# Expert outputs scattered with addition into two sums, and transposes and products sized by an expert's tokens

## What is computed

```python
logits = x @ gate_w.T; scores = softmax(logits)
topk_w, topk_ids = top_k(scores, K);  topk_w /= topk_w.sum(-1)
buf[e, pos] = x[tok]                       # up to CAP = 256 tokens of an expert, the rest is dropped
g, u = split(buf @ w13);  eo = (silu(g) * u) @ w2
routed[tok] += eo[e, pos] * topk_w         # four terms for each of the 1024 tokens
out = residual + routed + (silu(x @ sh_gate) * (x @ sh_up)) @ sh_down
```

## Time and profile before

| | us |
|---|---|
| median of 3 runs | 205.45 (204.16 to 205.67) |
| span of the profiled execution | 228.0 |
| head, to the first product of an expert | 0 to 82.1 |
| expert stage on PE | 82.1 to 197.5 |
| last scatters on POOL and their landing | 197.5 to 203.4 |
| tail: load, sums, stores | 203.4 to 228.0 |

### The profile page before, as it was taken

The page is one execution under the profiler, slowest core; times in us unless marked ns, Lnnn a source line. Parts: engine busy times, 40 slices in busy tenths (PEclk is TensorE's granted clock), DMA queues, the critical chain, the costliest instruction groups (busy, mean ns, idle before and its releaser), DMA issues.

```text
span 228.0 us, 3659 instructions
## 1 busy us (share of the span) xinstructions
PE 139.5 (61%) x819; PEld 119.8 (53%) x819; DVE 120.4 (53%) x385; ACT 84.8 (37%) x254; POOL 115.6 (51%) x140
## 2 busy tenths in 40 slices
PE   1124887787774879969895948858499479200000
PEld 0112765676663559959794837837398377100000
DVE  2878999997433344555253531536237055303990
ACT  3165678566563024434214231335225032002410
POOL 6201156888877500754563736555464646632740
PEclk9999996555555799988999788999979958755555
DMA  5999999998222264775775657465665731129930
GB/s 173 334 340 340 338 339 364 365 373 301 96 99 95 95 198 134 235 204 153 218 198 176 192 161 220 136 189 158 185 172 171 232 115 52 43 69 359 385 122 23
DMA packets 40270, 46.46 MB, mean 204 GB/s; under 512 B 4585, under 2 KB 37045, under 8 KB 40252
## 3 DMA queue, kind: packets, MB, share of 16 engines
q1 hardware_dynamic: 35200, 37.30, 53.2%
q0 software_dynamic: 4608, 8.54, 10.5%
q10 hardware_dynamic: 444, 0.40, 0.5%
HBM read 27.95 MB, written 22.45 MB: 221 GB/s over the span
## 4 chain that ended last, share of the span: by engine, by line
PE 36%; issue 20%; SPq 19%; another core or an unknown queue 7%; DVE 7%; DMA 5%; ACT 2%; POOL 0%; POOLq 0%; ACTq 0%; DVEq 0%
PE bank L882 18%; PE bank L899 11%; SPq L204 10%; PE bank L874 8%; SPq L227 5%; DVE part L769 4%; DMA G<-rows_out 3%; DVE act_t L730 1%; ACT xT L476 1%; DMA xg<-rows_in 1%; ACT sg L481 1%; DVE res L769 1%; SPq L210 1%; DMA rows_out<-yo,pick_idx 1%
## 5 line engine op out<-in xcount | busy, mean ns | idle before, releaser
L333 POOL DMA_INDIRECT rows_out<-yo,pick_idx x64 | 62.6, 978 | 55.7 <-issue 47.8
L882 PE MATMUL bank<-xT,w13b 128*128 128x128 f32 x368 | 51.6, 294 | 8.5 <-issue 5.6
L882 PEld LDWEIGHTS bank<-xT,w13b 128*128 128x128 f32 x368 | 48.1, 208 | 11.0 <-issue 11.0
L476 ACT ACTIVATE xT<-bank,cols 128x256 f32<-128x256 f32 x64 | 26.8, 473 | 43.0 <-PE bank L874 37.0
L899 PE MATMUL bank<-w_all,act_t 128*128 128x256 f32 x92 | 29.7, 434 | 16.0 <-DVE act_t L730 14.9
L730 DVE TENSOR_TENSOR act_t<-sg,bank 128x256 f32<-128x256 f32 x32 | 13.5, 421 | 49.3 <-ACT sg L481 36.5
L318 POOL DMA_INDIRECT rows_in<-n_row,slot_all x32 | 32.5, 1015 | 10.0 <-issue 10.0
L481 ACT ACTIVATE sg<-bank 128x256 f32<-128x256 f32 x32 | 12.3, 386 | 44.6 <-PE bank L882 25.1
L899 PEld LDWEIGHTS bank<-w_all,act_t 128*128 128x128 f32 x92 | 16.5, 209 | 18.8 <-issue 17.9
L737 DVE COPY yo<-bank 128x512 f32<-128x512 f32 x32 | 22.0, 687 | 6.6 <-remote 3.3
L874 PE MATMUL bank<-ident,xg 128*128 128x128 f32 x128 | 22.0, 301 | 1.3 <-DMA xg<-rows_in 1.2
(11 more groups left out here) (109 smaller groups left out, 194.3 us busy)
## 6 DMA issues: line engine op xcount, KB each, us to landing
rows_in<-zeros SPq DMA_DIRECT2D x32, 264.0 KB, 6.4
xg<-rows_in SPq DMA_DIRECT2D x32, 264.0 KB
w13b<-in_L_ffn_w_dram SPq DMA_DIRECT2D x32, 256.0 KB
w_all<-in_L_ffn_w_dram SPq DMA_DIRECT2D x4, 1024.0 KB
G<-rows_out SPq DMA_DIRECT2D x7, 512.0 KB, 7.1
rows_out<-yo,pick_idx POOLq DMA_INDIRECT x64
x_all<-in_x_dram SPq DMA_DIRECT2D x1, 768.0 KB, 5.2
v_all<-in_ctx_dram SPq DMA_DIRECT2D x1, 768.0 KB, 7.6
```

The source lines that it names most:

```text
L333: pool.indirect_dma_start(rows_out, bass.IndirectOffsetOnAxis(ap=pick_idx[:, q, a:a + 1], axis=0), yo[:, q, a, :], None, bounds_check=PICK ...
L476: act.activation(xT[:, j, h, :], FX[j][:, h, :], ACT.Copy, scale=nw[:, h:h + 1]).then_inc(s["f_x"], 1)
L882: last = nc.tensor.matmul(FG[q % 2][:, a, cols], w13b[q][:, h, a, :], xT[:, q % 2, h, cols], start=(h == 0), stop=(h == HC - 1))
```

## The change

**Sums.** `rows_out` is gone. `sums` holds two accumulators of 1280 rows: 256 spare rows (`SPARE`) and one row for each of the 1024 tokens. The first accumulator's token rows are set by storing `base_all` there, its spare rows and the whole second accumulator by zeros. A row in `rows_in` now carries its four experts, its four exponentials, their reciprocal sum (`NORM`) and its row in `sums` (`ROW`): 266 numbers. DVE weighs the down product with two factors when it takes it out of PSUM, and POOL scatters it with `compute_op=ALU.add`, expert e into accumulator e % 2. Slots without a token add zeros to a spare row, so all 256 rows of an expert are now moved. Before expert e POOL waits until the scatters of e-2 have landed. The tail loads both sums (2 MB), adds them, and stores four times 256 KB; weights, ACT and POOL have no part in it.

**Buffers.** All of `w13` stays in SBUF: it is loaded in the head, 8 MB in eight DMAs, mixed with the four of `w2`. `yo[e]` lies over `w13` of expert e, so it waits for no scatter. `xg` has six buffers. The last 32 rows' down product is kept in `w2_all`, and one store at the end replaces 32. The zeros lie in `xT`; ACT therefore waits for `sums_zeroed`. The `Fori` loops are gone: every engine's code is written out.

**PE.** Transposes of the second half are in a `pe.If`. Gate and up products have three widths, 128, 192 and 256 columns, by two bit masks that are loaded once.

```diff
-            for q in range(WB):
-                load_weights(q, q)
+            for g in range(EARLY):
+                load_w13(g)
+                if g % 2 == 0:
+                    load_w2(g // 2)
+            sp.dma_start(sums[0:SPARE].rearrange("(p a) c -> p (a c)", a=2), zero_rows).then_inc(sums_zeroed, 16)
+            sp.dma_start(sums[ACC:2 * ACC].rearrange("(p n a) c -> p n (a c)", p=P, a=2),
+                         zero_rows.unsqueeze(1).to_broadcast([P, ACC // (2 * P), 2 * C])).then_inc(sums_zeroed, 16)
...
+            for e in range(XB):
+                load_rows(e)
+            sp.wait_ge(s["sh_b"], B // 2)
+            sp.dma_start(sums[SPARE:ACC].rearrange("(b p) c -> p b c", p=P), base_all[:, :, :]).then_inc(base_stored, 16)
+            for e in range(E):
+                if e + XB < E:
+                    sp.wait_ge(s["f_xt"], e + 1)
+                    sp.wait_ge(s["f_yo"], e + 1)
+                    load_rows(e + XB)
...
             def scatter_out(e, q):
-                pool.wait_ge(s["pick_ready"], e + 1)
                 pool.wait_ge(s["f_yo"], e + 1)
-                pool.sem_inc(s["held_pool"], 1)
+                if e >= ACCS:
+                    pool.wait_ge(row_out[(e - ACCS) % YB], 32 * ((e - ACCS) // YB + 1))
                 for a in range(2):
-                    pool.indirect_dma_start(rows_out, bass.IndirectOffsetOnAxis(ap=pick_idx[:, q, a:a + 1], axis=0),
-                                            yo[:, q, a, :], None, bounds_check=PICKS - 1, oob_is_err=False)\
-                        .then_inc(row_out[q], 16)
+                    pool.indirect_dma_start(sums, bass.IndirectOffsetOnAxis(ap=pick_idx[:, e, a:a + 1], axis=0),
+                                            yo[e][:, a, :], None, compute_op=ALU.add).then_inc(row_out[q], 16)
...
-            with pool.Fori(0, E // WB) as i:
-                for q in range(WB):
-                    scatter_out(WB * i + q, q)
+            pool.wait_ge(sums_zeroed, 32)
+            pool.wait_ge(base_stored, 16)
+            for e in range(E):
+                scatter_out(e, e % YB)
...
-                dve.tensor_copy(yo[:, q, :, :], FY[q % 2]).then_inc(s["f_yo"], 1)
+                for a in range(2):
+                    last = dve.tensor_scalar(yo[e][:, a, :], FY[e % 2][:, a, :], owned[:, e, a:a + 1],
+                                             xg[e % XB][:, a, NORM:NORM + 1], ALU.mult, ALU.mult)
+                last.then_inc(s["f_yo"], 1)
...
+            for c in range(B // 2):
+                dve.wait_ge(sum_in[c], 16 * ACCS)
+                dve.tensor_tensor(G[0][:, 2 * c:2 * c + 2, :], G[0][:, 2 * c:2 * c + 2, :], G[1][:, 2 * c:2 * c + 2, :],
+                                  ALU.add).then_inc(s["res_ready"], 1)
...
+            def rows_to_channels(e, j, second):
+                pe.wait_ge(xg_in[e % XB], 16 * (e // XB + 1))
                 with pe.If(second != 0):
+                    transpose_half(e, j, 1)
+                transpose_half(e, j, 0).then_inc(s["f_xt"], 1)
...
+                with pe.If(third != 0):
+                    gate_up_slots(e, j, CAP)
+                with pe.Else():
+                    with pe.If(second != 0):
+                        gate_up_slots(e, j, MORE)
+                    with pe.Else():
+                        gate_up_slots(e, j, P)
```

388 lines of the change are left out of this document (172 added, 216 removed).

## The result

The changed kernel takes 250.42 us, median of 4 runs (249.56 to 252.31). The kernel before took 204.81 us beside it, median of 4 runs (203.62 to 205.67). The ratio is 1.223, with a 95% interval from 1.213 to 1.232. The prediction was 185 us and "faster": wrong in sign, and the time lies outside its range.

What follows compares the result with a forecast made beforehand. No single engine bounds the kernel; POOL's scatters decide after the change. Scatters from 96 us plus 95.3 land at 191.3; a 14.1 us tail gives 205.4 us of span, times 0.901 is 185 us, range 172 to 210.

Steps and rivals of the forecast that it cites:

- Scatters, D: POOL in the expert stage: time of one adding scatter, taken as 0.97 us like a plain one, at most 1.46.
- L: Expert stage: time from the end of a pair of scatters to its landing, taken as 3.5 us, between 2.5 and 5.0.
- dearer descriptors: Rival on POOL's scatters: a third descriptor for each row makes one 1.46 us; 203.7 us, no change; chance 0.15.
- Sum, the factor 0.901: Whole kernel: the runs' 205.45 us over the profile's 228.0 us, used to turn 205.4 us of span into 185.
- More transfers in the head: Head: 8.9 MB more ahead of the first rows; PE starts the experts at 88 us, 5.9 us late.
- When scatters can start: Start of the stage's scatters: POOL waits for the base_all store (94.7 us) and the first output (95.7); 96 us taken.
- PE: Expert stage: PE's work falls from 75 to 65 us, waits halve, PE ends about 173; none reaches the end.
- PE keeps its waits: Rival on the expert stage: PE's 40 us of waits stay and PE ends at 193; 192.5 us; chance 0.08.
- landing hidden: Rival on the stage's scatters: landing takes 2.8 us or less, so POOL only issues; 174.5 us; chance 0.15.
- Slow landing: Rival on the stage's scatters: landing takes 6.4 us, slower than before from 4.9 us; 227 us; chance 0.12.
- Tail: From the scatters' landing to the end: 2.1 MB loaded, last addition, stores; 14.1 us in place of 24.6.

Runs made afterwards that it cites:

- the kernel of that sum: Changed kernel with rows of 272 floats, one more iota at POOL's end, and plain scatters in place of adding ones: 208.13 us, ratio 1.008.
- the late iota: One more iota on POOL behind its last scatter; in the changed kernel with rows of 272 floats 238.38 us, ratio 1.024; alone, 249.50 us.
- the mended head: Changed kernel with rows of 272 floats and one more iota at POOL's end: 238.38 us with adding scatters, 208.13 us with plain ones.
- the first plain run: Changed kernel, rows still of 266 floats, with plain scatters in place of adding ones: 231.73 us, ratio 0.994.

## Why the prediction was wrong, step by step

- *Scatters, D.* The step that decided: "I take 0.97, the only scatter that has rows, and keep 1.46 for a rival". D is 1.55 us, above the upper bound, and the point at which the kernel gets slower was put at 1.49. Worth 29.7 us of POOL's chain. By itself this would not have carried the time out of the range: the prediction's own sum with D of 1.55 and L of 2.3 gives 96 + 60 x 1.85 + 7.1 + 2.3 + 14.1 = 230.5 us, by its factor 207.7 us. It takes the next two steps as well. The rival *dearer descriptors* had the right place and too small a size (its 212.0 should read 211.8, which changes nothing). Its reason does not hold: 16 rows cost 1.34 us and 128 rows 1.55, so the price is not written row by row. What POOL does in the 0.59 us more is open. That adding DMAs take a second read descriptor for each piece, as the Trainium skill says on the page quoted there, fits in direction, not in size, what the queue shows: 10752 packets against 4608 with plain scatters, so 144 a scatter in place of 48. The DMA engines pay in the same proportion: a share of 0.62 for one adding scatter each 1.85 us, 0.30 for one plain scatter each 1.26 us, so about three times as much for each. POOL's time, 1.6 times as long, goes with neither.
- *Sum, the factor 0.901.* The second step that failed: "I carry a result over by that factor". The 228.0 us of the profile and the 205.45 us of the runs differ in the stage of before, by waits and a lower clock, and the changed kernel shows neither on either kind of chip. Without the factor the sum is 205.4 us; the kernel of that sum took 207.4 us of span beside 206.0 for before. So even with D as taken the forecast should have been "the same", and without the factor there was no room for a D above 0.97 at all. This step made 20 us.
- *More transfers in the head.* PE started at 100.88 and not at 88. The count of bytes was right: with 272-float rows and the late iota PE starts at 88.6 and 88.9, held by the full queue and not by POOL, as the step said. Two edits priced at nothing were not free: two floats more in a row (9.1 us of time in this kernel, 18.1 in the other) and POOL's start (some 4 us once the rows are mended). The second follows from what the change takes away from POOL's end, which no row of before shows.
- *When scatters can start.* 111.93 in place of 96; 99.1 and 99.8 with the head mended. Most of the 3 us that remain are PE's clock. In the kernel with adding and the mended head it was at the lower of its two levels (1.2 GHz) while the first products of gate and up ran, where before had the upper one (2.4 GHz); ahead of them PE had been idle at times, waiting for the rows. They took 2.92 us, and 1.47 us for the same later. From PE's first transposes to the end of the first output it was 9.7 us, and 7.4 us in the kernel with 272-float rows alone, where PE's clock was at the upper level. There the other half of the term shows: POOL waits for the store of `base_all` until 102.42, 8.8 us behind PE's start, where the prediction had 6.7. The products and the window of the kernel with the mended head:

```profile
91.29 2.92 PE L858 MATMUL bank<-xT,w_all 128*128 128x192 f32 x8 [0.73 <-ACT xT L476]
...
97.31 1.47 PE L858 MATMUL bank<-xT,w_all 128*128 128x192 f32 x8
...
91.00:94.00 3.00, 2.71 (x8) 2.63 (x9) 0.00 (x0) 0.44 (x2) 0.00 (x0) 0.50 0.74 264
```

- *PE.* Predicted end 85 us behind its start; it was 78 us. The waits fell by more than half, and PE ended 55 us ahead of POOL, as the step said that nothing of it would reach the end. The rival *PE keeps its waits* is out for the changed kernel; the first plain run shows that it was a real one on some chips. The extra branches cost nothing that shows.
- *L.* At the end, on quiet DMA, 236.05 - 233.75 = 2.3 us from the last scatter to the landing seen. In the stage it was up to 5.6 us (pair ended at 165.45, next but one started at 171.02). With D of 1.55 two experts take 4 x 1.85 = 7.4 us to issue, which hides an L up to 7.4 - 3.45 = 3.95 us. So the landing was almost hidden, as in the rival *landing hidden* but because D had grown: of the 121.8 us 118.4 are issue. *Slow landing* did not come about; its 6.4 us was not the longest landing but the median of one kind of transfer.
- *Tail.* Predicted 14.1 us with its wakes; from 236.05 to 248.8 it took 12.8.

The sum by measured terms: 111.9 + 121.8 (64 scatters to 233.75) + 2.3 + 12.8 = 248.8. Against the prediction's 205.4: 15.9 from the start, 28.8 from D and L (124.1 against 95.3), -1.3 from the tail. Against the forecast of 185 us the factor adds its 20.

## What to carry to other kernels

Before you give an instruction the price of its nearest relative, ask which engine's work the new option changes, and let the bound be open upwards: here one keyword made each scatter 60% dearer on the engine whose queue ended last. A factor between a profile and the runs may be used only for a stretch that the change leaves alone; find first in which stage the two differ. Look at the row length in bytes when a field is added to a row, and at what an engine executes last, since its next execution starts from there.

## What the runs showed of the hardware

- An adding indirect DMA costs POOL 1.55 us for 128 rows of 1024 bytes, 1.55 for 128 rows of 512, 1.32 to 1.34 for 16 rows; a plain one of 128 rows 0.96. It makes 10752 - 4608 = 6144 more packets for 64 of them, 96 each.
- Zeros written as rows of 1064 bytes: 218 and 239 GB/s over two windows; of 1056 or 1088 bytes: 340 to 350, at the same DMA share (1.12, 1.13).
- POOL's first iota waits 8.7 to 12.1 us when the execution before ended with the all-reduce and scatters, and 0.3 us when it ended with an iota. An all-reduce waits 5.7 to 6.7 us, in before as well.
- The kernel before takes 205 to 207 or 232 to 234 us by the chip, the whole difference in its expert stage.
